# Router logits with the tokens as held tile, inverse products behind later shared steps, first low parts on GpSimd

## The reference

```python
probs = softmax(x @ W_router)            # 8 experts (L1, L3), 16 (L2)
top_v, top_i = top_k(probs, 2)
gate = sum(one_hot(top_i) * top_v)
y = sum over experts of expert(x) * gate + shared(x)
```

## Time and profile before

| | |
|---|---|
| timed runs, us | 3252.43, 3248.23, 3252.01 (median 3252.01) |
| profiled execution, us | 3249.07 |
| its span, first to last instruction, us | 3247.2 |
| mean granted clock of PE | 0.925 of full |
| PE busy | 2851.0 us, 88% of the span |
| DVE busy | 2224.1 us, 68% |
| ACT, POOL busy | 1501.5 us (46%), 1519.3 us (47%) |

### The profile page before, as it was taken

How to read it: one execution, slowest core, us unless ns; L and a number is a source line. 1 busy time by engine, 2 the same in 40 slices (tenths; PEclk the granted TensorE clock), 3 DMA queues, 4 the chain that set the end, 5 groups by cost and what they waited for, 6 DMA issues and landing times.

```text
span 3247.2 us, 60357 instructions
## 1 busy us (share of the span) xinstructions
PE 2851.0 (88%) x20922; PEld 2551.9 (79%) x20922; DVE 2224.1 (68%) x6074; ACT 1501.5 (46%) x3245; POOL 1519.3 (47%) x1487
## 2 busy tenths in 40 slices
PE   8979999999999899895798986769997868976898
PEld 6869999999999788794586975757776756966697
DVE  6767777777777668665735666578886765665665
ACT  3355566656666523344523434445554434443342
POOL 2345555555565305534600445568884445350034
PEclk9989999999999899897798987879998979989899
DMA  4022122121212300363004333810002552650533
GB/s 151 1 70 72 56 66 61 54 70 56 72 56 71 102 22 20 99 222 108 20 0 178 95 118 114 246 37 2 2 2 86 163 146 82 195 193 0 214 95 104
DMA packets 147766, 285.81 MB, mean 88 GB/s; under 512 B 20673, under 2 KB 70209, under 8 KB 144385
## 3 DMA queue, kind: packets, MB, share of 16 engines
q1 hardware_dynamic: 113458, 211.38, 19.5%
q0 software_dynamic: 21216, 57.96, 6.6%
q10 hardware_dynamic: 12816, 12.78, 1.2%
HBM read 191.59 MB, written 90.45 MB: 87 GB/s over the span
## 4 chain that ended last, share of the span: by engine, by line
PE 67%; DVE 17%; ACT 5%; issue 3%; DMA 3%; POOL 3%; SPq 0%; ACTq 0%; DVEq 0%; POOLq 0%
PE bank L552 18%; PE bank L553 17%; PE bank L554 17%; PE bank L2548 3%; PE bank L2564 2%; PE bank L1286 2%; POOL YG L1743 2%; PE bank L1005 1%; PE bank L1308 1%; DMA YG<-dyo,POSI 1%; DMA MXG<-dxn,IDX 1%; PE bank L692 1%; PE bank L723 1%; DVE ST L603 1%; DVE DEN L2309 1%
## 5 line engine op out<-in xcount | busy, mean ns | idle before, releaser
L1731 POOL DMA_INDIRECT MXG<-dxn,IDX x250 | 237.4, 950 | 248.6 <-PE bank L1286 222.7
L1743 POOL DMA_INDIRECT YG<-dyo,POSI x192 | 186.2, 970 | 177.1 <-DMA dyo<-YS 107.2
L2695 POOL TENSOR_SCALAR SX<-SX,MN 128x256 f32<-128x256 f32 x256 | 233.4, 927 | 45.6 <-DVE MN L2626 45.5
L1575 POOL TENSOR_TENSOR SHL<-SGS,SHH 128x512 fp32r<-128x512 f32 x12 | 16.4, 1367 | 418.5 <-ACT SHH L1380 374.8
L2626 DVE CUSTOM_DVE_ANT_0 SX<-bank,FMASK 128x128 f32<-128x128 f32 (+1 forms) x512 | 156.2, 350 | 49.0 <-PE bank L2539 48.9
L1104 POOL TENSOR_TENSOR HL<-HID,HH 128x512 fp32r<-128x512 f32 x56 | 72.3, 1290 | 240.7 <-ACT HH L1069 240.6
L552 PE MATMUL bank<-MWH,GH 128*128 x500 | 170.8, 342 | 0.9 <-DVE HB L1648 0.8
L1416 ACT ACTIVATE GH<-bank 128x256 fp32r<-128x256 f32 x250 | 95.5, 384 | 139.4 <-PE bank L1286 138.8
L554 PE MATMUL bank<-MWH,GL 128*128 x500 | 155.2, 310 | 0.0
L553 PE MATMUL bank<-MWL,GH 128*128 x500 | 155.1, 310 | 0.0
L2598 ACT ACTIVATE PT<-bank 128x384 f32<-128x384 f32 x256 | 111.6, 490 | 79.8 <-PE bank L2548 79.6
(11 more groups left out here) (464 smaller groups left out, 11633.5 us busy)
## 6 DMA issues: line engine op xcount, KB each, us to landing
dyo<-YS SPq DMA_DIRECT2D x250, 128.0 KB
RAW<-in_wheads SPq DMA_DIRECT2D x68, 320.0 KB, 6.1
BB<-dgates SPq DMA_DIRECT2D x68, 256.0 KB, 3.6
GB<-dgates SPq DMA_DIRECT2D x68, 256.0 KB, 4.2
RAW<-in_eL SPq DMA_DIRECT2D x32, 304.0 KB, 2.8
dkeptL<-MWL SPq DMA_DIRECT2D x32, 304.0 KB, 2.6
dkeptL<-MWH SPq DMA_DIRECT2D x32, 304.0 KB, 5.0
MWH<-dkeptL SPq DMA_DIRECT2D x8, 1216.0 KB, 12.7
```

Source lines behind the costliest of these rows:

```text
L1731: nc.gpsimd.indirect_dma_start(MXG[:, n % XGS, :], None, dxn, bass.IndirectOffsetOnAxis(ap=IDX[:, b:b + 1], axis=0)).then_inc(x_in[n % XGS ...
L1743: nc.gpsimd.indirect_dma_start(YG[:, i % YGS, :], None, dyo[0:m.blocks * P, :], bass.IndirectOffsetOnAxis(ap=POSI[:, c * NT + t:c * NT + t ...
L2695: nc.gpsimd.tensor_scalar(part, part, MN[:, n % RING2, 1:2], None, ALU.subtract).then_inc(s_less1, 1)
```

## The change

1. **Logits.** `logits_sum`, `logits_high`, LGS, HALVES and their two semaphores go. `moe_logits` now holds 128 tokens and moves the 16 columns of router weights past them, as `mm3` over both feature halves: 6 products for a tile, 24 for a group, 96 for a stage, straight into VectorE's bank. In `front_tensor` group g's logits stand behind the turn (and the warm products) of group g + 2; for an MoE stage from group 2 on all of them wait for the top-2 search two groups before, where only the sum did. In a tail the logits stay at `front_of(g)` + 3 and the search moves from + 4 to + 3.
2. **Prefix, places, slots.** `moe_prefix` runs halfway through up(0); places and slots stand ahead of the first gated product on VectorE.
3. **Inverse products and hot chunks.** The inverse products stand behind up(3) and up(4) (gated) or up(3) and up(5). Hot chunk 0 stands behind step 0, 1 behind step 1, 2 and 3 behind step 2; the index behind step 4 or 5.
4. **Low parts.** In cached stages GpSimd makes SHL of steps 0 to 3, in the others of 2 and 3 as before.

```diff
         def moe_logits(pe, st, p):
 
             pe.wait_ge(xt_lo, st.tr * HALF + p + 1)
-            if p >= 2:
-                pe.wait_ge(lg_sb, HALF * st.rt + p - 1)
-            o = bank[p % 2][0:32, 0:2 * P]
-            for k in range(KC):
-                x = slice(p * 2 * P, (p + 1) * 2 * P)
-                nc.tensor.matmul(o, RWS[:, st.router, k, 0:32], XTH[:, k, x], start=k == 0, stop=False)
-                last = nc.tensor.matmul(o, RWS[:, st.router, k, 32:64], XTL[:, k, x], start=False, stop=k == KC - 1)
-            last.then_inc(logits, 1)
-
-        def logits_sum(pe, st, p):
-
-            pe.wait_ge(lg_sb, HALF * st.rt + p + 1)
             g = p // 2
             if st.kind == 'moe' and p % 2 == 0 and g >= 2:
                 pe.wait_ge(r_tops, GROUPS * st.moe + g - 1)
             o = bank[LOGITS[g % 2] if st.kind == 'moe' else LOGIT]
-            for q in range(2):
-                t = 2 * p + q
-                last = nc.tensor.matmul(o[:, t * 16:(t + 1) * 16], LGS[:, p % 2, q * P:(q + 1) * P], HALVES[:, :],
-                                        start=True, stop=True)
+            for t in (2 * p, 2 * p + 1):
+                for k in range(KC):
+                    last = mm3(o[:, t * 16:(t + 1) * 16], xt(k, t * P, P), (RWS[:, st.router, k, 0, :], RWS[:, st.router, k, 1, :]),
+                               k == 0, k == KC - 1)
             last.then_inc(r_logits, 1)
...
         def front_tensor(pe, st):
...
-                if st.routed and 2 <= g < GROUPS:
-                    moe_logits(pe, st, 2 * g - 4)
-                    moe_logits(pe, st, 2 * g - 3)
-                if st.routed and 3 <= g < GROUPS:
-                    logits_sum(pe, st, 2 * g - 6)
-                    logits_sum(pe, st, 2 * g - 5)
                 if g < GROUPS:
                     front_turn(pe, st, 2 * g)
                     front_turn(pe, st, 2 * g + 1)
...
-                if st.routed and g >= GROUPS:
-                    logits_sum(pe, st, 2 * g - 6)
-                    logits_sum(pe, st, 2 * g - 5)
+                if st.routed and g >= 2:
                     moe_logits(pe, st, 2 * g - 4)
                     moe_logits(pe, st, 2 * g - 3)
...
+        INVERSE_AT = {True: (3, 4), False: (3, 5)}
+
+        def low_by_pool(st, s):
+
+            return s < LOWS_BY_VECTOR + 2 and (st.cached or s >= LOWS_BY_VECTOR)
...
             for s in range(m.early):
-                shared_up(pe, st, s)
-                if s == 0:
-                    moe_prefix(pe, st)
-                if s in (2, 3):
-                    moe_inverse(pe, st, 2 * s - 4)
-                    moe_inverse(pe, st, 2 * s - 3)
+                shared_up(pe, st, s, moe_prefix if s == 0 else None)
+                if s in INVERSE_AT[m.gated]:
+                    n = 2 * INVERSE_AT[m.gated].index(s)
+                    moe_inverse(pe, st, n)
+                    moe_inverse(pe, st, n + 1)
                 if s:
                     shared_down(pe, st, s - 1)
...
             moe_gaps(dve, st)
+            moe_places(dve, st)
+            moe_slots(dve, st)
             for s in range(m.early):
                 shared_product(dve, st, s)
-                if s < LOWS_BY_VECTOR or s >= LOWS_BY_VECTOR + 2:
+                if not low_by_pool(st, s):
                     shared_low(dve, nc.vector, st, s)
                 if s == 0 and st.name == 'L3':
                     nc.vector.tensor_scalar(SGT[:, :], SGT[:, :], 0.5, None, ALU.mult)
-                if s == 0:
-                    moe_places(dve, st)
-                    moe_slots(dve, st)
-                if s == 1:
-                    moe_hot(dve, st, 0)
-                    moe_hot(dve, st, 1)
+                if s < 2:
+                    moe_hot(dve, st, s)
                 if s == 2:
+                    if m.J == 2:
+                        shared_add(dve, st, 0)
                     moe_hot(dve, st, 2)
-                if s % m.J == 0 and s:
-                    shared_add(dve, st, s // m.J - 1)
-                if s == 2:
                     moe_hot(dve, st, 3)
-                if s == 3:
+                if s == 3 and m.J == 3:
+                    shared_add(dve, st, 0)
+                if s == (4 if m.gated else 5):
                     moe_index(dve, st)
                     moe_experts(dve, st)
+                if s > 3 and s % m.J == 0:
+                    shared_add(dve, st, s // m.J - 1)
```

More of the change, by code:

```diff
@@ L257, in build @@
         RWR = r.put('RWR', [P, 4, KC, 16])
-        MCR = r.put('MCR', [P, 3 * P + 2 * NT + 16 * NT + 16])
+        MCR = r.put('MCR', [P, 3 * P + 2 * NT + 16 * NT])
         r = Region(xn0, a0)
@@ L300, in build @@
         YG = r.put('YG', [P, YGS, D])
-        LGS = r.put('LGS', [32, 2, 2 * P])
-        assert tables_end <= r.at
+        r = Region(max(r.at, tables_end), a1)
         TOP = r.put('TOP', [P, NT, 8])
@@ L585, in tables_vector @@
                 nc.vector.memset(SIZES[:, 2 * m.router + 1:2 * m.router + 2], float(m.base))
-            nc.vector.memset(RWS[:, :, :, 48:64].bitcast(F32), 0.0)
-            nc.vector.tensor_copy(RWS[:, :, :, 0:16], RWR[:, :, :, :]).then_inc(consts, 1)
+            nc.vector.tensor_copy(RWS[:, :, :, 0, :], RWR[:, :, :, :]).then_inc(consts, 1)
             dve.wait_ge(consts, 3)
-            nc.vector.tensor_copy(RWS[:, :, :, 32:48], RWR[:, :, :, :])
-            nc.vector.tensor_tensor(RWS[:, :, :, 16:32], RWR[:, :, :, :], f32(RWS[:, :, :, 0:16]), ALU.subtract).then_inc(consts, 1)
+            nc.vector.tensor_tensor(RWS[:, :, :, 1, :], RWR[:, :, :, :], f32(RWS[:, :, :, 0, :]), ALU.subtract).then_inc(consts, 1)
         def twice(a):
@@ L684, in front_scalar @@
                         front_store(act, st, g)
-                if st.routed and g >= 2:
-                    logits_high(act, st, 2 * g - 4)
-                    logits_high(act, st, 2 * g - 3)
         def warm(n, b):
@@ L1203, in logits_sum, with shared_up @@
             o = bank[LOGITS[g % 2] if st.kind == 'moe' else LOGIT]
-            for q in range(2):
-                t = 2 * p + q
-                last = nc.tensor.matmul(o[:, t * 16:(t + 1) * 16], LGS[:, p % 2, q * P:(q + 1) * P], HALVES[:, :],
-                                        start=True, stop=True)
+            for t in (2 * p, 2 * p + 1):
+                for k in range(KC):
+                    last = mm3(o[:, t * 16:(t + 1) * 16], xt(k, t * P, P), (RWS[:, st.router, k, 0, :], RWS[:, st.router, k, 1, :]),
+                               k == 0, k == KC - 1)
             last.then_inc(r_logits, 1)
[L1210 to L1217, removed]
+        def shared_up(pe, st, s, between=None):
             m = st.m
@@ L1224, in shared_up @@
                 for k in range(KC):
+                    if between and (u if m.gated else k) and not (k if m.gated else u):
+                        between(pe, st)
                     col = m.shared_at[j] + (u * KC + k) * P
@@ L1341, in moe_tensor @@
             nx = st.next
-            for k in range(m.front_of(GROUPS - 1) + (5 if nx else 1)):
+            for k in range(m.front_of(GROUPS - 1) + (4 if nx else 1)):
                 for g in range(GROUPS if nx else 0):
@@ L1450, in moe_scalar @@
                         front_high(act, nx, 2 * g + 1)
-                    if k == done + 3 and nx.kind == 'moe':
-                        logits_high(act, nx, 2 * g)
-                        logits_high(act, nx, 2 * g + 1)
                     if k == done + 1:
@@ L1572, in shared_low @@
             queue.wait_ge(hh_done, st.steps + s + 1)
-            if s in (LOWS_BY_VECTOR, LOWS_BY_VECTOR + 2):
+            if 0 < s < st.m.early and low_by_pool(st, s) != low_by_pool(st, s - 1) or s == st.m.early:
                 queue.wait_ge(h_ready, st.steps + s)
@@ L1697, in moe_vector @@
                 for g in range(GROUPS if nx and nx.kind == 'moe' else 0):
-                    if k == m.front_of(g) + 4:
+                    if k == m.front_of(g) + 3:
                         moe_tops(dve, nx, g)
@@ L1720, in moe_pool @@
             for s in range(m.early):
-                if LOWS_BY_VECTOR <= s < LOWS_BY_VECTOR + 2:
+                if low_by_pool(st, s):
                     shared_low(pool, nc.gpsimd, st, s)
@@ L3099 @@
     q['moec'] = np.concatenate([p[:, None] < p, np.ones((P, P)), np.broadcast_to(p, (P, P)), p[:, None] + P * tile,
-                                np.broadcast_to(P * tile, (P, NT)), np.broadcast_to(np.tile(tile > 0, 16), (P, 16 * NT)),
-                                p[:, None] % 16 == np.arange(16)],
+                                np.broadcast_to(P * tile, (P, NT)), np.broadcast_to(np.tile(tile > 0, 16), (P, 16 * NT))],
                                axis=1).astype(np.float32)
```

11 lines of the change are left out of this document (1 added, 10 removed).

## The result

The changed kernel takes 3287.38 us (median of 4, 3282.66 to 3289.78) against 3252.22 before: ratio 1.0103, interval 1.0087 to 1.0120, so 35 us slower. Its profiled span is 3280.8 us, 33.6 more than before, at a mean granted clock of 0.917.

The account below looks back on a forecast made before the run. TensorE was taken as the bound, with 67% of the chain; fronts +46, products behind L0#2's front +1, tails +4, constants' copies -0.4, early sections -24 sum to +27 us: 3277 us, 8 in 10 within 3243 to 3298.

Parts of the forecast that it names:

- the fronts: Six stretches from last warm product to first up product: 18.0 us each in place of 61.97 in all, +46 us.
- the products behind L0#2's front: Up products after L0#2's front, which today runs at full clock, start at half clock: about +1 us.
- the tails: Logits inside the stages before L2#1 and L3#1: +4 us ahead of L2#1, 0 ahead of L3#1.
- the early sections: First up product to the 24 warm products ahead of the experts, six stages: -33 us, net -24 after clock falls.
- The price of the narrow product: Logits product of 16 columns on 128 held: 0.115 us at full clock, 0.214 at half, 24 to a group.
- The f16 price: Lower bound for a logits product, from the f16 inverse products: 0.025 us a start; excluded by the prediction.
- second rival: Down(0)'s wait drops the clock in all six stages and fronts fall at 4.0 us: +43, about 3293 us; chance 0.15.
- the gather: In L2#1, GpSimd's gather was to come some 7 us earlier against the first up product, as SHL(3) comes earlier.
- Two signs: Inverse products waiting under 5 us in all; the wait for SHL grown, most of it at down(0).
- The held clock: First rival: clock holds in the fronts, 6 x 12.0 us; -13, about 3239; faster once four hold; chance 0.11.
- The moved wait: Another name for the second rival: the wait only moves, to down(0); +43 us, about 3293; chance 0.15.
- The replay: L1#2's early section stepped through: down(0) waits 2.3 us, down(3) 2.6, the inverse wait goes; 35.2 us, saving 3.9.

Follow-up runs that it names:

- the run with 128 columns: Changed kernel with each MoE-stage logits product moving 128 router columns past the held tokens in place of 16, L0's fronts unchanged: 3262.67 us, ratio 1.0042 to the kernel before.
- the logits alone: Kernel before with only the new logits (part 1), early sections in their old order: 3305.98 us, ratio 1.0179.
- the early changes alone: Kernel before with only parts 2 to 4 of the change, logits as before: 3236.7 us, ratio 0.9962.

## Why the prediction was right

The measured 3287.38 us lies 10 above the forecast and at the upper end of the 3266 to 3288 that the forecast alone was given. The steps were right in kind. Against its terms the fronts cost 0.7 us more, the products behind L0#2's front 1.2, the tails 2.6, and the early sections gave 5.9 less.

**The price of the narrow product.** Taken from the sum's records at 0.115 and 0.214 us; the starts are 0.111 and 0.213 apart. The f16 price was rightly left out. By the Trainium skill ("TensorE: Matmul & The Clock Gate", "LDWEIGHTS (loading the stationary operand)") a load's time is its columns over 1.2, in ns, without the clock: an estimate of 107 ns for 128 columns. The distance of the starts agrees at full clock and is twice that at half (the load's own record lasts 0.19 and 0.33 us), and the measurement decides. The prediction sends this price to its second rival; it belongs to the first, since by it the fronts would cost as little at half clock as at full.

**The clock in the fronts.** A front was put at 18.0 us with a fall some 4 us behind the last warm product, +46 us for six. They measure 17.4 to 18.7, +46.7. The reason, little moved past freshly held tiles, was argued from two falls; the run with 128 columns shows it. The figure for a front that never falls, 12.0, came out as 11.7. The stretch of products behind L0#2's front lost 2.2 us for the 1 forecast (75.4 for 73.2; 1.1 with the logits alone).

**The tails.** +4 in the tail ahead of L2#1 measures +4.7 (from L1#2's last early product to L2#1's first up), and +4.6 with the logits alone. The 0 ahead of L3#1 measures +1.9, but not for the logits: 1.9 with the early changes alone, 0.1 with the logits alone.

**The early sections.** -24 forecast, -18.1 measured. L1#1 gave 3.0 of 5.2, L2#2 7.1 of 6.8, L3#1 2.0 of 2.4. In the cached stages the clock does fall behind the wait for down(0), as taken, and in L1#1 and L2#1 too, which was not; but for 3.4 us each and not 7, so L1#2 gave 2.3, not 0.5 (L3#2 1.7 of 2.4). The length of the wait alone does not decide it: down(0) waits 2.31 us in L3#1 and in L3#2, and behind it the clock (seventh number) stays up in the one and is down in the other:

```profile
2722.30:2727.00 4.70, 4.56 (x25) 3.79 (x26) 3.93 (x8) 0.67 (x2) 0.00 (x0) 1.00 0.00 0
3079.80:3083.10 3.30, 3.30 (x10) 2.63 (x9) 3.23 (x4) 0.63 (x1) 1.46 (x1) 0.50 0.26 109
```

The step that was mis-sized is L2#1: the gather comes 2.6 us earlier against its first up product, not 7, and the section is 2.0 shorter. There down products still wait 4.3 us once for SHL on VectorE, the inverse products 3.1, and the prefix 2.0 for VectorE's step behind the picks (TD). Two signs came out only in part: the inverse products wait 5.3 us in all and not under 5, and of the 18.8 us by which the wait for SHL grew down(0) has 9.8, half and not most.

**Where two errors met.** 46.7 + 2.2 + 6.6 - 18.1 is 37.4 us; the spans differ by 33.6. The rest, -3.8, is in the stretches between (the one with attn0 2.0 shorter, L2#1's experts with attn2 3.7). Over the twelve profiled executions, with nearly the same code there, the first takes 1097.8 to 1104.7 us and the second 500.3 to 504.0, so an effect of this size cannot be told from chance. That it brought the total nearer to the forecast is luck.

**The rivals.** The held clock did not come by itself. The run that brings it to four fronts saves 25 us in them and some 20 in all, and is slower than before by 0.4% still. That four were enough for faster was wrong by the prediction's own prices: 4 x 12.0 + 2 x 18.0 - 62.0 is +22, which with the tails only cancels the -24 of the early sections. In that run L0's two fronts still lose 9 and 10 us, and the early sections give 15.4. The moved wait is half real: five of the six stages fall behind down(0), near that rival's case, though for half the time. With the inverse products moved alone the moved wait takes the whole gain; the change avoids that by moving places and slots as well. The replay that put down(0) at 2.3 us (2.93) and down(3) at 2.6 (2.23) had this right, without saying that it hung on that part.

## What to carry to other kernels

Where PE is the bound, a product's price is what it holds and at which clock: exchanging which operand is held can keep every wait hidden and still lose, if each fresh load is followed by few moving columns. Here, with 16, PE stayed full and its clock was 0.59 to 0.64 in the mean of a front, and with 128 it was 1.00. Read the granted clock stage by stage before and after, and if such products are needed, move more columns past each tile while that is free. And a wait that goes when work is moved back should be looked for at the next consumer on the same engine: here it needed two moves together to shrink, from 76.8 to 51.1 us, and it did not go.

## What the hardware showed that was not expected

At full clock a float32 product on 128 freshly held columns starts 0.11 us behind the last whether it moves 16 columns or 128; the front with 128 took 11.7 us at 1.00, the one with 16 took 17.9 at 0.61. Products that do no useful work made a front faster (144 in 16.6 us against 96 in 17.4). And with them the fall is not the same from front to front: 3.4 to 14.5 us behind the last warm product for one and the same stream of PE; what decides between these stays open.
